# PE's slot begins with the next gate product; weight preparation behind the variance; a table of its own for the last chain; four gate buffers

## What is computed

```python
# block 1, on layer-normed x, for 4 chunks x 4 batches
xi, z = split(x @ in_proj.T);  xc = silu(causal_conv4(xi) + conv_b)
dt, Bs, Cs = split(xc @ x_proj.T);  dt = softplus(dt @ dt_proj.T + dt_proj_b)
h = exp(dt * A) * h + (dt * xc) * Bs      # over 256 tokens, 16 states
y = (sum_s h_s * Cs_s + xc * D) * silu(z);  out = y @ out_proj.T + skip * x
x = x + layer_norm(out) @ proj.T + proj_b
# block 2, t = layer_norm(x) by token
logits = t @ router.T;  top 2 of 16, softmax over the two -> combine
x = x + sum_e combine_e * (silu(t @ Wg_e) * (t @ Wu_e)) @ Wd_e     # F = 256
```

## Time and profile before

| | |
|---|---|
| median of 3 runs | 334.9 us (333.28 to 337.46) |
| the profiled execution | 334.86 us, its span 333.1 us |
| busy over the span | PE 290.8 (87%), DVE 238.1 (71%), POOL 168.4 (51%), ACT 152.4 (46%) |
| mean granted TensorE clock | 0.969 |
| chain that ended last, by engine | PE 44%, issue 28%, POOL 14%, DVE 8%, ACT 4% |

### The profile page before, as it was taken

How to read it: one execution, slowest core, us unless ns; L and a number is a source line. 1 busy time by engine, 2 the same in 40 slices (tenths; PEclk the granted TensorE clock), 3 DMA queues, 4 the chain that set the end, 5 groups by cost and what they waited for, 6 DMA issues and landing times.

```text
span 333.1 us, 3808 instructions
## 1 busy us (share of the span) xinstructions
PE 290.8 (87%) x1172; PEld 212.2 (64%) x1172; DVE 238.1 (71%) x380; ACT 152.4 (46%) x228; POOL 168.4 (51%) x155
## 2 busy tenths in 40 slices
PE   7986799989699989876699887688899998699996
PEld 5842645545355767654576766466678786588885
DVE  2479899999586976989769769877864364355543
ACT  2578755535453337564333376533423562222221
POOL 5000898886338566877498659765821220322310
PEclk9999769999979999999979999979999999999999
DMA  7991666337822864655748666641110200221110
GB/s 262 349 281 39 201 211 201 126 126 202 191 85 78 200 186 129 186 143 135 212 107 224 173 145 171 157 130 64 47 37 28 63 31 4 63 80 48 48 32 16
DMA packets 21748, 43.39 MB, mean 130 GB/s; under 512 B 2848, under 2 KB 8032, under 8 KB 21728
## 3 DMA queue, kind: packets, MB, share of 16 engines
q1 hardware_dynamic: 16848, 34.09, 36.1%
q10 hardware_dynamic: 4880, 9.07, 9.5%
HBM read 42.03 MB, written 1.11 MB: 130 GB/s over the span
## 4 chain that ended last, share of the span: by engine, by line
PE 44%; issue 28%; POOL 14%; DVE 8%; ACT 4%; DMA 1%; POOLq 0%; DVEq 0%; ACTq 0%
PE bank L730 17%; POOL y L311 7%; PE bank L911 7%; PE bank L878 7%; PE bank L896 7%; POOL u L304 5%; PE bank L734 3%; DVE y L567 2%; POOL xs L318 2%; DMA X<-x 1%; ACT th L500 1%; PE bank L792 1%; ACT bank L438 1%; DVE dt L571 1%; DVE y L576 1%
## 5 line engine op out<-in xcount | busy, mean ns | idle before, releaser
L500 ACT ACTIVATE th<-bank,cst 128x512 f32<-128x512 f32 x64 | 44.0, 687 | 131.6 <-PE bank L878 131.5
L304 POOL TENSOR_TENSOR u<-dtx,BCs 128x512 f32<-128x512 f32 x64 | 81.0, 1276 | 15.3 <-DVE h L624 14.6
L896 PE MATMUL bank<-xs,Wu 128*128 128x256 f32 x256 | 67.9, 388 | 21.6 <-DVE hid L694 15.1
L686 DVE SCALAR_TENSOR_TENSOR th<-th,bank 128x512 f32<-128x512 f32 x64 | 43.9, 686 | 59.4 <-ACT th L500 59.2
L318 POOL TENSOR_TENSOR xs<-xm,Gs 128x512 f32<-128x512 f32 x32 | 41.0, 1283 | 83.5 <-DMA Gs<-CE_far 79.3
L896 PEld LDWEIGHTS bank<-xs,Wu 128*128 128x128 f32 x256 | 47.5, 192 | 37.9 <-issue 20.8
L878 PE MATMUL bank<-xm,Wg 128*128 128x256 f32 x256 | 67.5, 387 | 0.0
L911 PE MATMUL bank<-hid,Wd 128*128 128x256 f32 x256 | 67.0, 386 | 0.0
L438 ACT ACTIVATE bank<-dt,cst,A 128x510 f32<-128x510 f32 x64 | 49.6, 775 | 20.1 <-DVE h L624 17.8
L878 PEld LDWEIGHTS bank<-xm,Wg 128*128 128x128 f32 x256 | 49.8, 195 | 7.5 <-issue 0.5
L911 PEld LDWEIGHTS bank<-hid,Wd 128*128 128x128 f32 x256 | 48.5, 192 | 8.5 <-issue 2.1
(11 more groups left out here) (120 smaller groups left out, 220.1 us busy)
## 6 DMA issues: line engine op xcount, KB each, us to landing
BCs<-BC_far SPq DMA_DIRECT2D x72, 256.0 KB, 4.1
Gs<-CE_far ACTq DMA_DIRECT2D x32, 256.0 KB, 3.4
BCs<-BC_far SPq DMA_DIRECT2D x56, 128.0 KB, 3.1
Wg<-gate_w SPq DMA_DIRECT2D x1, 2048.0 KB, 10.7
Wu<-up_w SPq DMA_DIRECT2D x1, 2048.0 KB, 16.2
par<-params ACTq DMA_DIRECT2D x1, 597.5 KB, 4.4
X<-x SPq DMA_DIRECT2D x2, 256.0 KB, 4.7
BC_far<-BC_rows SPq DMA_DIRECT2D x4, 128.0 KB, 3.0
```

What stands on the lines that cost most here:

```text
L304: g.tensor_tensor(u[:, k % U_RING], dtx[:, k // NS, :], BCs[:, k % BC_RING, 0], ALU.mult)\
L500: a.activation(th[:, n % 2], bank[gate_bank(n)][:], ACT.Tanh, scale=0.5, bias=zero).then_inc(S["th_r"], 1)
L686: v.scalar_tensor_tensor(th[:, n % 2], th[:, n % 2], 1.0, bank[gate_bank(n)][:], ALU.add, ALU.mult)\
L896: o = t.matmul(bank[up_bank(n)][:, f * T:(f + 1) * T], Wu[:, e, f * P:(f + 1) * P], xs[:, pr % 2, ts], start=True, stop=True)
```

## The change

- In slots: PE issues gate(n+1) first, then up(n), the chain item, down(n-2). gate(0) goes from behind the first 28 steps into step 27; it waits for step 24 rather than 25.
- Start: 11 instead of 8 fillers ahead of the centred x; the variance products go ahead of the five weight products; 4 instead of 16 fillers before the input projection.
- In the first 28 steps the filler is left out in steps 24 and 25 too.
- The last chain (batch 3, slots 36 to 45) takes its slots from a table of its own, `BESIDE_TAIL`, and requests the first gates of its batch itself.
- `Gs` has four tiles; requests are issued one pair sooner.

```diff
-G_RING = 3
+G_RING = 4
+BESIDE_TAIL = {"DVE": {0: "gated", 2: "norm", 4: "tokens", 5: "top", 6: "mix"},
+               "PE": {0: "total", 1: "out", 2: "var", 3: "centre", 4: "var_t", 5: "logits", 7: "turn", 8: "x1"},
+               "ACT": {1: "sq", 2: "rstd", 3: "sq_t", 4: "rstd_t", 6: "exp", 7: "gates", 8: "x1", 9: "spread"}}
...
-            table = (BESIDE_STEPS if b == 1 else BESIDE_ITEMS)[engine]
+            table = (BESIDE_STEPS if b == 1 else BESIDE_TAIL if b == BATCH else BESIDE_ITEMS)[engine]
...
                 if item == "spread":
-                    spread_gate(0)
-                    spread_gate(1)
+                    spread_gate(b * E // 2)
+                    spread_gate(b * E // 2 + 1)
+                    if b == 0:
+                        spread_gate(2)
...
-                if n % E == E - 2 and n + 2 < ITEMS:
+                if n % E == E - 2 and n // E < BATCH - 2:
                     spread_gate(n // 2 + 1)
-                pr = n // 2 + 2
-                if n % 2 == 0 and pr < ITEMS // 2 and 2 * pr % E:
+                    spread_gate(n // 2 + 2)
+                pr = n // 2 + 3
+                if n % 2 == 0 and pr < ITEMS // 2 and pr % (E // 2) > 1:
                     spread_gate(pr)
...
             pe.wait_ge(S["mean_c"], 1)
-            keep_warm(8, 6)
+            keep_warm(11, 6)
...
+            pe.wait_ge(S["const0"], 7)
+            for i in range(2):
+                pe.wait_ge(S["sq_r"], i + 1)
+                mm(bank[2 + i][:], var_in_w, half(sq, i), "var_r")
             pe.wait_ge(S["par_in"], 16)
             mm(bank[7][:, 0:P], p("out0"), M[:], "prep_r")
...
             mm(bank[6][:, 0:P], p("proj_t"), M[:], "prep_r")
-            pe.wait_ge(S["const0"], 7)
-            for i in range(2):
-                pe.wait_ge(S["sq_r"], i + 1)
-                mm(bank[2 + i][:], var_in_w, half(sq, i), "var_r")
...
-            keep_warm(16, 5)
+            keep_warm(4, 5)
...
-            for k in range(FIRST):
-                back(*chain("PE", k))
-                if k + 1 < FIRST:
-                    spread_c(k + 1)
-                if k:
-                    sum_state(k - 1)
-                if k < FIRST - 2:
-                    keep_warm(1, 7)
...
-                    pe.wait_ge(S["hc_r"], LAST_C2)
+                    pe.wait_ge(S["hc_r"], LAST_C2 - 1)
...
-            gate(0)
+            for k in range(FIRST):
+                if k == FIRST - 1:
+                    gate(0)
+                back(*chain("PE", k))
+                if k + 1 < FIRST:
+                    spread_c(k + 1)
+                if k:
+                    sum_state(k - 1)
+                if k < FIRST - 4:
+                    keep_warm(1, 7)
             for n in range(ITEMS):
                 k = step_at(n)
+                if n + 1 < ITEMS:
+                    gate(n + 1)
                 up(n)
                 back(*chain("PE", k))
                 if n >= LAG:
                     down(n - LAG)
-                if n + 1 < ITEMS:
-                    gate(n + 1)
                 if k - 1 < BY_PE:
                     sum_state(k - 1)
```

## The result

| | before | after |
|---|---|---|
| median | 334.25 us (runs beside it) | 301.81 us of 4 runs (301.19 to 303.66) |
| ratio | | 0.902, interval 0.895 to 0.910 |
| profiled execution, its span | 334.86, 333.1 | 303.66, 301.8 |
| mean granted clock | 0.969 | 0.982 |

The change is faster by 9.8%; 306.5 was forecast, with a range of 300 to 316. Lines have moved: L686 is now L692, L694 is L700, L878 is L875, L896 is L893, L911 is L908, L500 is L505, L318 is L321.

The account below looks back on a forecast made before the run. The middle stage was taken as bound by waits between DVE and PE, no engine full, and the end by PE. 334.86 - 2.0 (start) - 1.1 (gate(0)) - 17.8 (middle) - 7.4 (tail) = 306.56, stated as 306.5 us; range 300 to 316.

Parts of the forecast that it names:

- gate(0): Before item 0: gate(0) in step 27 and two fillers fewer take 1.1 us off its 2.71 us wait.
- The middle: The 36 slots with scan step and item: gate product first in PE's slot gains 17.8 us, bounds nothing and 23.7.
- rstd slots: Slots 6, 9, 22 and 25: tanh late by 0.4 to 0.7 us rather than 1.5, about 2.4 us remaining.
- slots 16 and 32: Where a new batch's gates arrive: request about 2 us sooner, up(16) still 1.3 us late, 2.6 for two.
- the walk: Slots 0 to 36 stepped through with the profile's durations: 121.9 us against 141.0, a gain of 19.1.
- the sum of the waits: Middle stage: DVE's 23.7 us of waits less 7.4 us that remain, a gain of 16.3 us.
- the tail's 7.4 us: From up(36) to the last down: table, early gates and four buffers cut 86.55 to 79.1 us; bounds 2.5 and 7.4.
- Table loads: The six rstd slots: about 2.7 us longer each by the skill's page; by the profile rows the sum stands.
- rival 4: ACT stands still again after each table load, 2 x 1.3 us more per rstd slot: 322.1 us; chance 0.01.
- The fourth tile: Fourth `Gs` buffer, gates asked one pair sooner: no gain of its own; without that cover a late pair costs up to 2.7 us.
- The start: Before the input projection: filler and variance-product edits, net between -2.9 and -0.3 us, taken as -2.0.
- Rival 2's sign: PE idle before the centre product, if ACT stays the bound in chain slots: 316.3 us; chance 0.08.

Follow-up runs that it names:

- the last one: Kernel after with three tiles, ACT's exp, gates and gate requests ahead of its decay, `sum_state` ahead of down in slots 0 to 4, weight products first: 299.34 us, 0.899.

## Why the prediction was right

**The middle: right in mechanism, 2.3 us too small.** The walk through the slots gave 121.9 us and the stage took 121.5. The places of the waits that remain were right too: rstd slots (0.26, 0.69, 0.21 and 0.69 us before L692 in the kernel after; forecast 0.4 to 0.7 each) and slots 16 and 32 (1.5 and 1.7 before `hid`; forecast 1.3 each). I had forecast 7.4 us of waits in the 36 slots; L692 waits 1.85 there and `hid` 4.6, together 6.5. The step that failed is the last one, where I took 17.8 between the walk (19.1) and the sum of the waits (16.3). These two rows show what the sum of waits leaves out, first from before, then after, both from L686 of item 0 to that of item 36:

```profile
102.86:244.44 141.58, 118.22 (x490) 91.08 (x489) 116.19 (x182) 67.00 (x101) 99.16 (x81) 0.98 0.55 147
```

```profile
99.01:220.54 121.53, 113.22 (x497) 91.52 (x496) 113.64 (x182) 69.20 (x102) 100.68 (x81) 1.00 0.65 172
```

DVE's idle time fell from 25.4 to 7.9 us, 17.5. Its busy time fell too, by 2.55 us, with the same 182 instructions. Records of DVE overlap when instructions follow at once. L686 at 105.78 lasts 0.68, to 106.46, and the scan behind it starts 0.08 sooner; behind an L686 that came after a wait (133.01, 0.69 long) the scan starts only as it ends. Both in the timeline of before:

```profile
106.38 1.23 DVE L624 TENSOR_TENSOR_SCAN bank<-bank,u 128x512 f32<-128x512 f32 x1
...
133.69 1.23 DVE L624 TENSOR_TENSOR_SCAN bank<-bank,u 128x512 f32<-128x512 f32 x1
```

So a late L686 loses 0.08 in front of it and most of 0.08 behind it, and neither is idle time. The lengths of all DVE records of the stage add up to 126.4 us before and 126.2 after; of these 10.2 overlapped before and 12.6 after. The scan started 0.02 or less before the end of L686 in 24 of the 36 slots before, and in 4 after. 17.5 + 2.55 is the 20.05 measured. The walk used distances from start to start, 2.92 a slot, and so did not lose it.

Two things that the text did not reckon are in the 20.05. The first is the clock. The granted clock was low in two stretches of the stage before (0.84 over 160 to 171 us, 0.83 over 214 to 224). The first of them stands at the 2.70 us in which PE waited for `xs` of slot 16, and all four profiles of the old order have one there; the second made slot 29 4.69 us, and with only the start changed it was absent and the slot took 3.01. None of the ten profiles of the new order has one in the stage. The stage took 141.6, 142.0, 140.2 and 140.3 us in the old order (before, table alone, start alone, order undone), against 118.0 to 122.0. Against the shorter old ones the gain is 18.7 to 18.8, and 17.8 was 1 us off.

The second is the write of the gates to DRAM. DMA issues of 156 to 158 us in the kernel before:

```profile
CE_far<-CE ACTq DMA_DIRECT2D x1, 16.0 KB, 3.8
```

I had put the request of 160.72 behind ACT's tanh and decay alone. The write of 156.94 landed at 160.70, so with tanh early the request could still not have left before that. It left 2.0 us behind the write in the kernel after (146.44 to 148.40) only because the write now took 1.4 us. The 2 us that I counted on came true by this luck at slot 16 (3.8 between write and request, now 2.0); at slot 32 the two lay 3.1 apart before and 2.9 now, and the slot grew from 4.07 to 4.76.

The long slots 16 and 32 of the kernel after also hide how much the order brought. By itself it took the stage from 141.58 to 118.89 us, 22.7 and not 17.8; the kernel after gave 2.6 of that back, 2.2 of it in these two slots. That the walk's 121.9 met the 121.5 is luck to that extent.

**PE's order: right, and larger than its place in the sum.** I gave the tail's 7.4 us to the denser table and the earlier gates. The total was right to 0.1 (79.1 forecast, 79.0 measured), and up(48) begins at 257.61 without a wait; but 6.6 of it came with the order, 0.9 with the table. The table alone is slower. What in my text made the difference is the clause that each chain item is ready when PE comes to it: true behind a gate product, and not without one.

**Table loads.** The next activation in the tail comes 1.30 us after a load began in the kernel after as well (229.35, then 230.65), and rival 4 falls: the rstd slots cost DVE 0.2 to 0.7 us, not 2.6 more. The Trainium skill's drain of 1.38 us behind a load ("ScalarE: Activation LUTs", What ACT_TABLE_LOAD costs) shows in no trace here: in each of them the next activation comes 1.29 or 1.30 us after the start of the load in 11 to 13 of 17 cases.

**gate(0).** 0.8 us of 1.1: L692 of item 0 waits 1.85 rather than 2.71, so exactly one group of PE (0.86) was gained, in all ten profiles with this edit against the four without. The filler of step 25 gave nothing.

**The fourth tile: put at nothing, and still open.** I counted only the benefit of asking a pair sooner. There is no benefit to see: with three tiles the median is the same. In the profiled execution slots 16 and 32 took 2.4 us more than with three tiles, of which slot 32's part goes with the late write of the gates and not with the third request.

**The start: 3.0 rather than 2.0, and most of it by the clock.** Three steps from 16.41 to 13.40 can be read from the profiles. The x products at the upper level (1.95 us against 3.75) are worth 2.4: 16.41 to 14.01, the latter with no edit of the start. I had named this as something that may come; my reason, that PE had paused before them, does not hold, since in two profiles they ran at the upper level behind pauses of 0.73 and 0.90. Fewer fillers before the projection are worth 1.4: 14.01 to 12.61, where 1.8 was reckoned. The order of the weight products, which I put at nothing, costs 0.8: 12.61 to 13.40. DVE's queue decides there and not ACT's root. The delay of 0.7 by three more fillers did not come, since 22 filler matmuls took 4.37 us and not the 5.2 that I had reckoned, and the x products began no later than before (5.51). That the sum landed 1.0 beside the forecast is luck in part: it depends on which level the profile of before happened to have.

**What would have shown it.** L692 waits 3.7 us (under 8 was asked) and the 36 slots take 121.5 (124). One sign that I named was wrong: tanh still waits for the gate product by the trace, 23.6 us at L875. ACT is mostly idle and follows PE at once; its wait costs nothing, since DVE comes later. Rival 2's sign, PE idle before the centre product, was absent in the new order.

## What to carry to other kernels

In a queue that works in order, put first the work whose inputs are oldest, when something long hangs on its result: one product moved ahead of three was 30 of 32 us, in a stage where no engine was full, and it also gave the cover that made a denser table harmless. Reckon a stage by walking slots from start to start, not by adding up the waits that the profile lists. Before putting a late request down to the engine that issues it, look when the transfer it depends on has landed. Two edits have to be priced in the order in which they will stand, for the table that was free behind the moved product cost 5.6 us of tail without it. And a start edit is not judged from one profile, if the clock alone moves it by 2.4 us.

## What was unexpected of the hardware

- 256 KB broadcasts from ACT's queue landed after 7.6 us at the median when four fell into 148 to 156 us beside SP's stream, and after 5.1 with three. Before, two at the same place took about 4.
- The write of a batch's gates to DRAM (16 KB, ACT's queue) landed after 1.4 us or after 1.9 to 3.9. For batch 1 it was 3.7 to 3.9 in all four profiles of the old order, 1.4 in the eight of the new one with ACT's order unchanged, and 3.3 in the two that issue it 2 us sooner. What it stands beside at that moment was not looked into.
- The moment at which PE's level rises after the start differs between executions: 22 filler matmuls took 4.37, 5.06, 4.21 and 4.23 us in four kernels with the same start (after, three tiles, weights first, the last one). In two kernels with 16 filler matmuls of 3.78 us each, the x products behind took 3.75 and 1.96, and the kernel before and the one with the table alone, whose starts are the same, differ by 2.4 us at the projection. The Trainium skill says the same of this moment ("TensorE: Matmul & The Clock Gate", Part 1).
- The granted clock of the 36 slots was 0.98 or 0.99 in the profiles of before and with the start alone, and 1.00 in those of the order alone and of the kernel after, with no stretch below it. In the new order PE pauses less there (113 of 121.5 us busy rather than 118 of 141.6). In PE's pauses of 2.6 to 2.8 us in the old order (slot 16, and two in the tail with the denser table), or within 2 us behind them, it was at the lower of its two levels each time; behind the pause of 2.50 before up(48) it was not.
- A memset that lasts 0.165 us on DVE made a slot longer by 0.08 to 0.14 only; most of the rest is the overlap with the next instruction.
